# A fused feature-sampling, linear-recurrence and mixture-of-experts kernel: the experts' last matmul turned round, with w3 as its stationary operand

## The reference

```python
logits = jnp.einsum('bsd,de->bse', x, gate_w) + gate_b
probs = jax.nn.softmax(logits, axis=-1)
top_probs, top_idx = jax.lax.top_k(probs, 2)
top_probs = top_probs / jnp.sum(top_probs, axis=-1, keepdims=True)
dispatch = jnp.sum(jax.nn.one_hot(top_idx, 16) * top_probs[..., None], axis=-2)
hidden = jax.nn.silu(einsum('bsd,edh->bseh', x, w1)) * einsum('bsd,edh->bseh', x, w2)
expert_out = jnp.einsum('bseh,eho->bseo', hidden, w3)
out = h + jnp.einsum('bseo,bse->bso', expert_out, dispatch)
```

## Time and profile before

| | |
|---|---|
| median of 3 runs | 2246.7 us (2244.17 to 2251.53) |
| the profiled execution: its time | 2242.19 us |
| its span (first to last instruction) | 2240.4 us |
| mean granted clock of TensorE | 0.954 of full |
| TensorE busy | 2017.2 us, 90% |
| VectorE busy | 1996.7 us, 89% |
| ScalarE busy | 942.2 us, 42% |
| GpSimd busy | 1454.0 us, 65% |

### The profile page before, as it was taken

How to read it: one execution, slowest core, us unless ns; L and a number is a source line. 1 busy time by engine, 2 the same in 40 slices (tenths; PEclk the granted TensorE clock), 3 DMA queues, 4 the chain that set the end, 5 groups by cost and what they waited for, 6 DMA issues and landing times.

```text
span 2240.4 us, 45957 instructions
## 1 busy us (share of the span) xinstructions
PE 2017.2 (90%) x15249; PEld 1837.6 (82%) x15249; DVE 1996.7 (89%) x6209; ACT 942.2 (42%) x2040; POOL 1454.0 (65%) x1657
## 2 busy tenths in 40 slices
PE   2468999989898999999899998989999998999899
PEld 1356789889798988889798897989888898988788
DVE  1257899999999999999999999999999999999998
ACT  1224443444444444444444444444444444433333
POOL 0388767578585858758575775858587685858700
PEclk9779999999999999999999999999999999998999
DMA  8787536466564646666463665746376674532200
GB/s 200 214 238 207 172 106 179 139 186 194 162 189 112 182 123 193 188 169 194 111 183 111 189 191 165 198 114 188 104 197 183 169 199 120 175 88 85 68 3 6
DMA packets 363145, 346.80 MB, mean 155 GB/s; under 512 B 49312, under 2 KB 313632, under 8 KB 362784
## 3 DMA queue, kind: packets, MB, share of 16 engines
q1 hardware_dynamic: 313760, 209.59, 34.8%
q0 software_dynamic: 49152, 134.28, 20.1%
HBM read 205.89 MB, written 137.89 MB: 153 GB/s over the span
## 4 chain that ended last, share of the span: by engine, by line
PE 60%; DVE 27%; issue 8%; POOL 2%; DMA 1%; ACT 1%; DVEq 0%; POOLq 0%; ACTq 0%
PE bank_o L637 15%; PE bank_h L628 10%; PE bank_h L629 9%; PE bank_d L693 9%; PE bank_d L703 7%; DVE ob L975 5%; DVE hid L964 4%; DVE wsam L1053 2%; DVE v_sb L1088 2%; PE bank_a L715 2%; PE bank_p L658 2%; POOL gath L574 2%; DVE v_sb L1081 2%; PE bank_p L657 1%; PE bank_p L663 1%
## 5 line engine op out<-in xcount | busy, mean ns | idle before, releaser
L574 POOL DMA_INDIRECT gath<-table,idx x1024 | 1127.0, 1101 | 271.4 <-issue 237.5
L637 PEld LDWEIGHTS bank_o<-w_sb,hid 128*128 128x128 f32 x4608 | 636.2, 199 | 75.4 <-issue 60.6
L637 PE MATMUL bank_o<-w_sb,hid 128*128 128x64 f32 x4608 | 630.8, 275 | 43.7 <-DVE ob L975 42.6
L628 PE MATMUL bank_h<-xsplit,w 128*128 128x384 f32 x1536 | 616.4, 401 | 28.3 <-DVE hid L964 27.7
L787 ACT ACTIVATE silu<-bank_h 128x384 f32<-128x384 f32 x768 | 380.6, 496 | 481.5 <-PE bank_h L629 476.5
L629 PE MATMUL bank_h<-xsplit,w 128*128 128x384 f32 x1536 | 532.0, 346 | 0.0
L975 DVE SCALAR_TENSOR_TENSOR ob<-bank_o,disp,ob 128x64 f32<-128x64 f32 x2160 | 474.5, 276 | 3.7 <-PE bank_o L637 3.4
L964 DVE TENSOR_TENSOR hid<-silu,bank_h 128x384 f32<-128x384 f32 x768 | 420.6, 548 | 25.1 <-ACT silu L787 18.2
L628 PEld LDWEIGHTS bank_h<-xsplit,w 128*128 128x128 f32 x1536 | 301.2, 196 | 59.4 <-DVE hid L964 35.2
L1053 DVE TENSOR_TENSOR wsam<-gath,cw 128x1024 f32<-128x1024 f32 x256 | 312.3, 1220 | 25.8 <-DMA gath<-table,idx 19.6
L693 PE MATMUL bank_d<-eye,wsam 128*128 128x128 f32 x2048 | 281.8, 283 | 30.1 <-DVE wsam L1053 26.6
(11 more groups left out here) (142 smaller groups left out, 1864.4 us busy)
## 6 DMA issues: line engine op xcount, KB each, us to landing
table<-pixmaj SPq DMA_DIRECT2D x80, 1024.0 KB, 10.0
xin<-x_dram SPq DMA_DIRECT2D x256, 256.0 KB
table<-pixmaj SPq DMA_DIRECT2D x32, 960.0 KB
table<-pixmaj SPq DMA_DIRECT2D x16, 1088.0 KB
gath<-table,idx POOLq DMA_INDIRECT x1024
out_dram<-ob SPq DMA_DIRECT2D x48, 96.0 KB
gath<-w_dram SPq DMA_DIRECT2D x4, 512.0 KB, 9.3
interp_sb<-interp_dram SPq DMA_DIRECT2D x1, 1024.0 KB, 5.5
```

Source lines behind the costliest of these rows:

```text
L574: pool.indirect_dma_start(out=gath[buf][:, p, :, :].rearrange("p a c -> p (a c)"), out_offset=None, in_=table[par], in_offset=bass.Indirec ...
L628: mm(bank[:, 0:GC], w12[:, e, which, 0, :], xsplit[gp][:], start=True, stop=False)
L637: last = mm(bank_o[n % 2][:, C * k:C * (k + 1)], hid[:, n % HB, 128 * k:128 * (k + 1)], w3_sb[:, e, :], start=True, stop=True)
```

## The change

Experts are taken in pairs (PAIRS = 8 a group). In W, w3 of the two experts is the stationary operand, 64 columns each, on the lower and the upper half of the array's columns; hid moves, 384 columns. The result, two experts' outputs stacked on the 128 partitions with tokens as columns, is in one bank_o. Since tokens now lie along the free axis, disp can no longer be a scalar per partition. So disp is turned on TensorE (P9, three transposes to 16 partitions), evicted by ScalarE into dispT, stored to DRAM (P10), and read back by eight transfers (R), one a pair, each of which spreads an expert's row of 384 weights over 64 partitions. All nine transfers are issued by ScalarE; the R wait until the store has landed. VectorE multiplies bank_o by that tile into one of five buffers scaled (W on VectorE, one 128x384 instruction a pair). After four pairs TensorE turns and sums them in bank_z (Z, 3 x 4 accumulating transposes of 128x128), and VectorE adds both column halves to ob (M2, two 128x192 instructions). All five ORDER strings are written anew; SyncE and GpSimd keep the same pieces and change places here and there.

```diff
+PAIRS = NE // 2
+HALF = PAIRS // 2
+SB = 5
...
+        disp_rows = [nc.dram_tensor(f"disp_rows{p}", [NE, GC], F32, kind="Internal").ap() for p in range(2)]
...
-        disp = [sb(f"disp{i}", [128, GT, NE]) for i in range(2)]
+        disp = sb("disp", [128, GT, NE])
+        dispT = [sb(f"dispT{i}", [NE, GC]) for i in range(2)]
+        wide = sb("wide", [128, PAIRS, GC])
+        scaled = [sb(f"scaled{i}", [128, GC]) for i in range(SB)]
...
-        bank_o = [ps(f"bank_o{i}") for i in range(2)]
+        bank_o, bank_z = ps("bank_o"), ps("bank_z")
...
                     elif kind == "W":
-                        g, e = args
-                        n = SLOTS * b + NE * g + e
-                        pe.wait_ge(hid_done, n + 1)
-                        wait(pe, eo_added, GT * (n - 1))
+                        g, q = args
+                        n = PAIRS * (NGRP * b + g) + q
+                        pe.wait_ge(hid_done, 2 * n + 2)
+                        wait(pe, eo_scaled, n)
+                        for h in range(2):
+                            last = mm(bank_o[C * h:C * (h + 1), 0:GC], w3_sb[:, 2 * q + h, :], hid[:, (2 * n + h) % HB, :],
+                                      start=True, stop=True)
+                        last.then_inc(eo_ready, 1)
+                    elif kind == "Z":
+                        g, half = args
+                        n = PAIRS * (NGRP * b + g) + HALF * half
+                        pe.wait_ge(eo_scaled, n + HALF)
+                        wait(pe, mix_v, 4 * (NGRP * b + g) + 2 * half)
                         for k in range(GT):
-                            last = mm(bank_o[n % 2][:, C * k:C * (k + 1)], hid[:, n % HB, 128 * k:128 * (k + 1)],
-                                      w3_sb[:, e, :], start=True, stop=True)
-                        last.then_inc(eo_ready, 1)
+                            for q in range(HALF):
+                                last = mm(bank_z[:, 128 * k:128 * (k + 1)], scaled[(n + q) % SB][:, 128 * k:128 * (k + 1)],
+                                          eye[:], start=q == 0, stop=q == HALF - 1, is_transpose=True)
+                        last.then_inc(mix_ready, 1)
+                    elif kind == "P9":
+                        g = args[0]
+                        pe.wait_ge(disp_done, NGRP * b + g + 1)
+                        for k in range(GT):
+                            last = mm(bank_p[0:NE, 128 * k:128 * (k + 1)], disp[:, k, :], eye[:], start=True, stop=True, is_transpose=True)
+                        last.then_inc(dispT_ready, 1)
...
+                    elif kind == "P9":
+                        g = args[0]
+                        act.wait_ge(dispT_ready, NGRP * b + g + 1)
+                        wait(act, eo_scaled, PAIRS * (NGRP * b + g - 1))
+                        copy(dispT[gpar(par, g)][:], bank_p[0:NE, 0:GC]).then_inc(dispT_stored, 1)
+                    elif kind == "P10":
+                        g = args[0]
+                        act.wait_ge(dispT_stored, NGRP * b + g + 1)
+                        wait(act, eo_scaled, PAIRS * (NGRP * b + g - 1))
+                        act.dma_start(disp_rows[gpar(par, g)], dispT[gpar(par, g)][:]).then_inc(disp_out, 16)
+                    elif kind == "R":
+                        g, q = args
+                        n = PAIRS * (NGRP * b + g) + q
+                        act.wait_ge(disp_out, 16 * (NGRP * b + g + 1))
+                        wait(act, eo_scaled, n - PAIRS + 1)
+                        rows = disp_rows[gpar(par, g)]
+                        act.dma_start(wide[:, q, :], bass.AP(rows.tensor, rows.offset + 2 * q * GC,
+                                                            [[GC, 2], [0, C], [1, GC]])).then_inc(wide_in[q], 16)
...
-                        wait(dve, eo_ready, n - HB + 1)
+                        wait(dve, eo_ready, (n - HB) // 2 + 1)
...
-                    elif kind == "Z":
-                        g, e = args
+                    elif kind == "W":
+                        g, q = args
+                        n = PAIRS * (NGRP * b + g) + q
+                        dve.wait_ge(eo_ready, n + 1)
+                        dve.wait_ge(wide_in[q], 16 * (NGRP * b + g + 1))
+                        wait(dve, mix_ready, (n - SB) // HALF + 1)
+                        tt(scaled[n % SB][:], bank_o[:, 0:GC], wide[:, q, :], ALU.mult).then_inc(eo_scaled, 1)
+                    elif kind == "M2":
+                        g, half = args
                         gp = gpar(par, g)
-                        n = SLOTS * b + NE * g + e
-                        dve.wait_ge(eo_ready, n + 1)
-                        if e == 0:
+                        n = 2 * (NGRP * b + g) + half
+                        mix.start(n)
+                        dve.wait_ge(mix_ready, n + 1)
+                        if half == 0:
                             wait(dve, out_done[gp], 8 * NGRP * b + 8 * (g - gp))
-                        for k in range(GT):
-                            if e:
-                                dve.wait_ge(eo_added, GT * (n - 1) + k + 1)
-                            stt(ob[gp][:, k, :], bank_o[n % 2][:, C * k:C * (k + 1)], disp[gp][:, k, e:e + 1],
-                                (ob[gp] if e else h2[g])[:, k, :], ALU.mult, ALU.add).then_inc(eo_added, 1)
+                        else:
+                            dve.wait_ge(mix_v, mix.value())
+                        both = bank_z[:, 0:GC].rearrange("p (k h c) -> p k h c", k=GT, h=2)
+                        link(mix, tt(ob[gp][:], both[:, :, 0, :], (ob[gp] if half else h2[g])[:], ALU.add))
+                        mix.inc(tt(ob[gp][:], both[:, :, 1, :], ob[gp][:], ALU.add))
```

206 lines of the change are left out of this document (108 added, 98 removed), and 6 rows, old and new, of the table KINDS.

## The result

| | before | after |
|---|---|---|
| median | 2248.1 us (2244.17 to 2251.53) | 3344.9 us (3329.27 to 3350.68) |
| ratio, 95% interval | | 1.487 [1.481, 1.493] |
| span of the profiled execution | 2240.4 us | 3348.8 us |
| a batch, by the index instruction | 128.1 us | 193.3 us |

The forecast was 2182 us in a range of 2080 to 2275. The kernel takes 1097 us longer than before and lies far above the worst case that was written down (2420).

A forecast was written before the change was run, and what follows sets the result against it. VectorE's load makes TensorE wait; TensorE's own work is only a few per cent shorter than the 128.1 us batch. Terms sum to -3.9 us a batch, -58 over 15, -63 with the end: 2179 profiled, 2182 us median, range 2080 to 2275.

The forecast's parts named there:

- VectorE's part: VectorE loses L975 instructions, gains multiplications and additions: -14.3 us a batch, 121 us become 107, no longer a bound.
- TensorE's part: W's pairs at 0.84 us save 8.2 us a batch, Z and P9 add 8.0: TensorE's work stays, -0.2.
- The waits won: TensorE's waits for ob (2.7 us a batch) and hid (1.3) vanish; half-clock stretch gives 1.7, short queueing behind VectorE 1.0.
- Transfers costed at nothing: R's reads add 75 MB, DMA share rises to about 0.71; gathers are issued at 85 us a batch, so no cost.
- ScalarE's part: ScalarE gains 3 evictions and 27 DMA issues a batch, rising from 42% to some 54% busy; runs of issues cost 3 us.
- I take 0.5 with the gap between two: Each DMA issue on ScalarE holds it for 0.5 us with the gap, 13.5 us a batch for 27 issues.
- The quickest small transfer took 1.9 us: ScalarE's wait for the store to land before a run of R: 1.9 us from issue to landing.
- I take 1 us a group, 3 us: Silus late behind ScalarE's runs of issues cost TensorE 1 us a group, 3 us a batch, within bounds 0 to 15.
- Slower through ScalarE's queue: Rival, 13%: ScalarE's issues meet a backlog as behind table stores; runs cost 15 us a batch, 2250 to 2360 us.
- issues of over 0.7 us in the mean: Sign in the new profile that the forecast is wrong: DMA issues on ScalarE last over 0.7 us in the mean.
- No overlap: Rival, 6%: W's two column halves don't overlap, a pair takes 1.6 us; 140 us a batch, 2420 us.
- The last sign of being wrong: TensorE below 93% with VectorE below 86% would say the order of pieces, not an engine, sets the time.

The follow-up runs named there:

- e4_none: The changed kernel without the store P10 and the transfers R, wide filled once with a constant, so no dispatch weights: 2154.2 us, ratio 0.959.
- e1_sixteen: The changed kernel with each R cut in two, one for each expert, slowest dimension 64 instead of 2: 2515.3 us, ratio 1.121.
- e10_early_two: The changed kernel with bf16 dispatch weights, wide double-buffered, two spreading transfers a group, two silus behind the store: 2297.2 us, ratio 1.020.
- e5_four: The changed kernel with four spreading transfers a group (64 partitions x 4 rows) instead of eight: 2285.3 us, ratio 1.019.
- e8_one_store: As e1_sixteen, but dispatch weights are stored for the first group only and every group spreads those: 2426.8 us, ratio 1.080.
- e9_half: As e1_sixteen, but only the first expert of each pair is spread, 24 issues a batch: 2271.6 us, ratio 1.012.
- e11_half_one_store: As e9_half, but dispatch weights are stored for the first group only and spread for every group: 2171.7 us, ratio 0.965.
- e13_first_two: As e10_early_two, but each group's spread goes in two parts, pairs 0 and 1 first, then 2 to 7: 2217.4 us, ratio 0.985.

## Why the prediction was wrong, step by step

**VectorE's part: right in direction, too large.** -14.3 us a batch was forecast. Between 300 and 1900 us VectorE was busy for 121.7 us a batch before and for 111.2 without transfers: -10.5. The per-line terms hold: taken line by line, the sum falls by 13.6 us. But different lines overlapped for 14.0 us a batch before and only for 10.9 without transfers. The L975 instructions had run partly beside others, so less busy time went with them than their own. VectorE isn't the bound, as said, at 91% instead of 86%.

**TensorE's part: right.** A pair at 0.80 us lies in 0.78 to 0.92, nearer the lower end than the 0.84 taken: 1.0 us a batch better. The halves start 7 ns apart, as the sign for overlap had it. Z at 1.40 us in the median instead of 1.19 is 1.3 us a batch worse. 96% busy was said, and is measured without transfers.

**The waits won: right in sum, not term by term.** Without ScalarE's term the sum gives 121.2 us a batch and 2134 us; e4_none has 122.5 and 2154. This half was 20 us too hopeful, and its terms erred both ways. TensorE's waits for ob and hid, 2.7 and 1.3 us a batch, were to vanish; 1.6 (now for the scaling, 21.0 us in 1600) and 0.6 are left. For the clock 1.7 us was taken. The granted clock rose from 0.97 to 1.00 between 300 and 1900 us, and TensorE's busy time fell from 120.9 to 117.8 us a batch, 3.1 us, though its work by the terms above is unchanged; so the clock seems to have given more. That the errors largely cancel is luck. (The last step of the sum is also off by 1.5: 2179 and 4.5 are 2183.5, not 2182. Nothing hangs on it.)

**Transfers costed at nothing: right for the gathers, wrong for their own landing.** Between 300 and 600 us the DMA share is 0.41 in after and 0.66 in e1_sixteen, below the 0.71 said, and wsam's idle time before it was 35.0 us in the whole of after. But the spread of e10_early_two or e5_four lands late once a batch (9.6 and 7.6 us a batch of VectorE's waits), which no term had. In after it isn't seen: VectorE hardly waits for the weights there, 11.4 us in the whole run.

**ScalarE's part: the step that failed**, in three terms.
- "I take 0.5 with the gap between two": the earlier trace rows shows issues of other shapes, 0.43 us for one alone and 3.96 behind a queue. The second was taken for a case of its own (behind table stores), and R's own shape, two experts and a repetition, was not asked about. Measured 3.9 us, 85 us a batch instead of 13.5. Of the 70.8 us a batch between e4_none and after, 49.4 go with this term alone (after against e1_sixteen, which even has twice the issues). With sixteen engines the kernel takes 2515 us instead of 3345.
- "The quickest small transfer took 1.9 us": the store's round trip is 3.3 us in the median from its issue to the first R, and 7 us where it meets table stores. With the store's own issues it costs 5.8 to 6.8 us a batch where nothing covers it (e1_sixteen against e8_one_store, e9_half against e11_half_one_store).
- "I take 1 us a group, 3 us": with the issue length and number that were assumed, e9_half measures 129.9 - 122.5 = 7.4 us, within the bounds of 0 to 15. The issues by themselves are 0.6 us. So with R's length as assumed the kernel would take about 2270 us by e9_half: inside the range, but slower than before. The sign of the forecast hung on the round trip, too.

**The rivals.** "Slower through ScalarE's queue" had the right place and chain (issue, silu, hid, bank_h), and the chance of 13% and the price of 15 us a batch were too small. Its mechanism, an issue held by a backlog of SyncE's table stores, isn't what is seen: in the kernels on sixteen engines no R on ScalarE lasts more than 1.9 us. The table stores show in the store's landing in one group of three, and the length of an R came from R's own shape. The price rested on a misreading, too: the 4.49 us in the earlier trace rows are both table stores of a pair, not one. Its sign, issues of over 0.7 us in the mean, is there: 3.5 us. "No overlap" fell by the 0.80 us. The last sign of being wrong, TensorE below 93% with VectorE below 86%, came true as well, but not its reading: e4_none has the same order of pieces and TensorE at 96%.

**What stays open.** It wasn't tried whether moving SyncE's table stores out of the way of the first group's store closes the 4.2 us a batch between e13_first_two and e4_none, where VectorE still waits 5.1 us a batch before a scaling. That the table stores cause the round trip of 7 us is read from timelines that fall together, not from an experiment. Nor did a run change the number of DMA engines and nothing else: e1_sixteen also cuts each R in two.

## What to carry to other kernels

Before a transfer that repeats a source (stride 0) is costed, write down its slowest dimension on both sides: if it is small, few DMA engines carry it (two here), and where several such transfers follow each other the issuing engine stands still (3.9 us each here, from the third on). A DMA issue on a compute engine is a piece of that engine's stream: add up one hold, with the wait for whatever it depends on, and compare it with what the engines behind it have in stock; here holds of some 4 us a group cost almost nothing, and what came on top nearly its full length. Where a store is read back at once, readers some pieces later and the first rows in a small transfer of their own helped here, by 4.8 and 5.2 us a batch.

## What the runs showed of the hardware

- A read of 128 x 1536 bytes with slowest dimension 2 held ScalarE for 3.9 us in the median and up to 10.9 (after); as two reads with slowest dimension 64, 0.62 us each (e1_sixteen). The first two of a group of eight took 0.5 us each in after: such an issue is short until two of its kind are ahead of it.
- An issue on ScalarE held it for 0.31 us (the store of 16 rows), 0.55 to 0.65 us (64 partitions), with one to eight rows a partition nearly alike (medians; e9_half with one row, e10_early_two with eight).
- DRAM written and read back: 3.3 us in the median from the store's issue to the start of the next issue that waits for it (after, e9_half), and up to 8.2 in after in the groups whose store meets table stores.
- Two fp32 matmuls of 384 columns on column halves overlapped almost fully: 0.80 us the pair (e4_none), changes of shape included; four passes of 384 columns without a change take 0.78.
